# Expert products as three float32r products, with the weights split into a high and a low part on the chip

## Chip, cores and metric

The kernel runs on one core of one Trainium2 chip. The metric is the device time of one execution, in microseconds (us), lower is better.

## The reference, cut to what matters

One layer: attention (4 sequences of 1024 tokens, 256 features, 16 heads of 16), and behind it a mixture of eight experts of which each token takes two, with a layer norm before and behind each half.

```python
x = x + _layernorm(attention(_layernorm(x), Wq, bq, Wk, bk, Wv, bv, Wo, bo))
xs = _layernorm(x).reshape(4096, 256)
dist = sqrt(max(|xs|^2 + |centroid|^2 - 2 xs @ centroid.T, 1e-12))
w, sel = top_k(dist, 2); w = softmax(w)             # we: (4096, 8), zero but for the chosen two
for e in range(8):                                  # Wg, W1: 256 x 684, W2: 684 x 256
    h = silu(xs @ Wg[e] + bg[e]) * (xs @ W1[e] + b1[e])
    out = out + we[:, e:e+1] * (h @ W2[e] + b2[e])
x = x + _layernorm(out)
```

All inputs and the output are float32.

## The kernel before, in words

Every engine runs its own written-out program; semaphores order them, and nothing is reordered. The stages follow one another: layer norm and q, k, v projections; attention; the output projection with both norms and the routing distances; the routing; the experts; the last norm.

**Attention** goes over 16 groups (batch and four heads), and a group over 16 units. For every unit PE makes four score products for the row maxima of a *later* group (`max_scores`, L1547, five units ahead), four score products for the softmax (`scores`, L1561), both in float32r, and `weigh` (L1574, float32). DVE reduces the maxima (`reduce_max`, L970 and L977), two halves of 1024 columns a unit. After eight units (half r of a group) the maxima are complete: POOL splits them (`split_max`: a cast L776, a subtraction L778), and DVE turns the result (`turn`, L983). `turn(g, 0)` stands in DVE's order between two reductions:

```python
            def max_pass(g, first=False):
                for m in range(UNITS):
                    reduce_max(g, m, 0)
                    if m == 0 and not first:
                        turn(g - 1, 1)
                    if m == ST:
                        turn(g, 0)
                    reduce_max(g, m, 1)
```

POOL's program in a group g is: `split_max(g + 1, 0)`, `split_max(g + 1, 1)`, `copy_values` for group g + 2 (L767; it waits until group g is weighed, so it runs some units into group g + 1), and in the groups 9 and 13 `norm_o` (two multiplications of 128 x 1024, L797) behind that. SP issues all DMAs of a group in a written-out order: the last result, the stacks and values of group g + 2, the rows of maxima of group g + 1, and at the end of the group's list a load that the later stages need (first weights `load_w1`, second weights `load_w2`).

**Projection and norms**: 16 steps of 256 rows; `norm_o` (L797) for batch 3 stands between two of POOL's additions `add_y` (L841), and waits for loads from `ot_scr` and `r_scr` that SP issues at step 4. PE's `project_o` waits for `norm_o`.

**Experts**: 71 tiles of 128 rows, each of one expert, whose number is read from `tile_e`. All weights and biases lie in SBUF. For a tile t, POOL gathers 128 rows (L852) and their weights (L866). PE turns the rows (`turn_rows`, L1703), makes gate and up (`gate_up`: four quarters of 342 columns, each of two float32 products, L1717), turns the 128 x 684 hidden values (`turn_hidden`, six transposes of 114 columns, L1727) and multiplies by the second weights (`down`, six float32 products of 256 columns, L1736). The trace has two MATMUL records for each float32 product, one for each float32r product and one for each transpose. DVE adds biases (L1208, L1211) and multiplies (L1216), ACT takes the silu (L1443), both save the turned hidden values (ACT L1454, DVE L1227), ACT scales the result (`save_y`, L1449), and POOL scatters it with addition into `y_d` (L859). PE's order in the loop is `gate_up(t)`, `turn_rows(t + 1)`, `down(t - 1)`, `turn_hidden(t)`.

**The last norm** reads `y_d` and a part of `x2_d` back: SP issues all twelve loads and only then reports the first (`s_back`), for which DVE's statistics (L1281) wait.

## Time and profile before

| | |
|---|---|
| runs of the kernel before | 1572.35, 1585.21, 1585.65 us; median 1585.21 us |
| the profiled execution | 1571.72 us, of it span 1569.9 us |
| mean granted TensorE clock | 0.956 |
| PE busy | 1428.5 us (91%) |
| DVE, ACT, POOL busy | 1107.7, 833.7, 430.8 us |
| moved by DMA | 141.82 MB, mean 90 GB/s |

The span is the time from the first to the last instruction. Busy times are sums over the engine's instructions; a PE that is busy by its records is not at its peak. PEld is the loading of stationary operands, which runs beside PE.

### The profile page before, as it was taken

To read this page: it belongs to the slowest core of one execution; us is meant where nothing else is said; L and a number is where in the kernel's file an instruction comes from. 1 tells how busy PE (TensorE), PEld (TensorE's weight loads), DVE (VectorE), ACT (ScalarE), POOL (GpSimd) and SP (SyncE) were. 2 spreads that over 40 slices of the span, in tenths; PEclk is the share of its full clock that TensorE was granted. 3 is DMA by queue.
4 is the path that set the end of the run, shared out by engine and by line. 5 is a ranking of instruction groups with operands and counts; after the bars stand their busy time and mean duration, and the time that the engine had idled before them with its cause. 6 is when DMAs were issued, how large, how long until landed. Compare 5 with 4: busy or idle time off the path is not lost.

```text
span 1569.9 us, 30203 instructions
## 1 busy us (share of the span) xinstructions
PE 1428.5 (91%) x9419; PEld 813.8 (52%) x9420; DVE 1107.7 (71%) x2101; ACT 833.7 (53%) x1613; POOL 430.8 (27%) x417
## 2 busy tenths in 40 slices
PE   7899999999999999999999259999999999999950
PEld 5454334333343433333455136777777777777740
DVE  6988999999999989997047764555554545555425
ACT  4523888888888878887956322222222222222215
POOL 5750000000000010001024143444444444444425
PEclk9998999999999999998999669999999999999985
DMA  6986274334646454540558804211221122122235
GB/s 209 257 225 116 69 171 98 59 81 68 96 64 126 65 90 65 94 79 16 159 91 204 281 25 95 33 30 33 33 33 33 31 33 33 30 33 33 33 92 193
DMA packets 125118, 141.82 MB, mean 90 GB/s; under 512 B 55131, under 2 KB 98949, under 8 KB 125030
## 3 DMA queue, kind: packets, MB, share of 16 engines
q1 hardware_dynamic: 109126, 121.98, 33.7%
q0 software_dynamic: 15904, 18.66, 7.2%
q8 instruction: 56, 0.92, 0.3%
q14 instruction: 32, 0.26, 0.1%
HBM read 86.30 MB, written 54.30 MB: 90 GB/s over the span
## 4 chain that ended last, share of the span: by engine, by line
PE 53%; DVE 36%; issue 6%; DMA 1%; POOL 1%; ACT 1%; SPq 1%; DVEq 0%; POOLq 0%; ACTq 0%
DVE mx L977 26%; PE psum L1717 21%; PE psum L1736 12%; DVE psum L970 4%; PE psum L1574 4%; PE psum L1547 3%; PE psum L1727 3%; PE psum L1561 2%; PE psum L1648 2%; PE psum L1521 1%; PE psum L1646 1%; PE psum L1507 1%; PE psum L1703 1%; PE psum L1667 1%; DVE work L1176 1%
## 5 line engine op out<-in xcount | busy, mean ns | idle before, releaser
L1366 ACT ACTIVATE work<-psum 128x512 f32<-128x512 f32 x1024 | 543.5, 600 | 92.1 <-PE psum L1561 67.1
L977 DVE TENSOR_REDUCE mx<-psum 128x1 f32<-128x1024 f32 (+1 forms) x512 | 547.2, 1097 | 23.6 <-PE psum L1547 10.5
L1547 PE MATMUL psum<-stack 48*128 48x512 f32 x1024 | 378.6, 451 | 19.6 <-DVE mx L977 8.8
L1561 PE MATMUL psum<-stack 50*128 50x512 f32 x1024 | 376.8, 453 | 0.0
L1717 PE MATMUL psum<-weights,values 128*128 x1136 | 340.6, 454 | 0.6 <-DVE values L1196 0.6
L1574 PE MATMUL psum<-work,values 128*32 128x384 f32 x4080 | 304.2, 394 | 0.2
L1547 PEld LDWEIGHTS psum<-stack 48*128 48x128 f32 x1024 | 162.7, 188 | 260.1 <-DVE mx L977 169.3
L1717 PEld LDWEIGHTS psum<-weights,values 128*128 128x128 f32 x1136 | 211.6, 191 | 98.8 <-issue 2.8
L1443 ACT ACTIVATE values<-values 128x342 f32<-128x342 f32 x142 | 69.3, 488 | 253.7 <-DVE values L1208 253.7
L1736 PE MATMUL psum<-weights,work 114*128 (+1 forms) x852 | 198.6, 383 | 1.1 <-ACT work L1454 0.8
L1561 PEld LDWEIGHTS psum<-stack 50*128 50x128 f32 x1024 | 162.4, 188 | 23.9 <-ACT work L1366 18.6
L1736 PEld LDWEIGHTS psum<-weights,work 114*128 114x128 f32 (+1 forms) x852 | 158.0, 192 | 21.1 <-issue 1.7
L1574 PEld LDWEIGHTS psum<-work,values 128*32 128x32 f32 x4080 | 89.4, 109 | 125.5 <-issue 103.3
L852 POOL DMA_INDIRECT values<-xn_d,at_x x71 | 70.0, 986 | 280.1 <-DVE at_w L1239 274.6
L1449 ACT ACTIVATE work<-psum,dots 128x256 f32<-128x256 f32 x71 | 33.6, 473 | 197.6 <-PE psum L1736 193.0
L1208 DVE TENSOR_TENSOR values<-psum,work 128x342 f32<-128x342 f32 x142 | 73.1, 515 | 92.3 <-PE psum L1717 64.2
L859 POOL DMA_INDIRECT y_d<-work,at_y x71 | 115.2, 1622 | 40.0 <-issue 27.2
L1211 DVE TENSOR_TENSOR values<-psum,work 128x342 f32<-128x342 f32 x142 | 73.1, 515 | 61.3 <-PE psum L1717 61.3
L1227 DVE COPY work<-psum 114x256 f32<-114x256 f32 x71 | 30.2, 425 | 117.8 <-PE psum L1727 117.8
L776 POOL CAST m<-mx 128x16 fp32r<-128x16 f32 x32 | 6.3, 198 | 365.4 <-DVE mx L977 365.4
L1216 DVE TENSOR_TENSOR values<-values 128x342 f32<-128x342 f32 x142 | 73.3, 516 | 14.7
L767 POOL TENSOR_TENSOR values<-weights,dots 128x512 f32<-128x512 f32 x16 | 20.5, 1283 | 227.0 <-issue 226.8
(185 smaller groups left out, 1266.8 us busy)
## 6 DMA issues: line engine op xcount, KB each, us to landing
stack<-qk_scr SPq DMA_DIRECT2D x192, 128.0 KB, 6.2
qk_scr<-weights SPq DMA_DIRECT2D x16, 1024.0 KB, 4.8
weights<-in_w SPq DMA_DIRECT2D x8, 1368.0 KB, 6.9
ot_scr<-weights SPq DMA_DIRECT2D x16, 512.0 KB, 3.2
weights<-in_w SPq DMA_DIRECT2D x8, 684.0 KB
work<-in_b SPq DMA_DIRECT2D x8, 684.0 KB, 8.7
y_d<-zeros SPq DMA_DIRECT2D x1, 4224.0 KB, 14.2
v_scr<-weights SPq DMA_DIRECT2D x32, 128.0 KB, 2.4
```

The costliest lines, as they stand in the source:

```text
L852: pool.indirect_dma_start(out=x_row, out_offset=None, in_=xn2_d, in_offset=bass.IndirectOffsetOnAxis(ap=at_x[:, 0:1], axis=0)).then_inc(s_ ...
L859: pool.indirect_dma_start(out=y_d, out_offset=bass.IndirectOffsetOnAxis(ap=at_y[:, 0:1], axis=0), in_=y_row, in_offset=None, compute_op=AL ...
L977: dve.tensor_reduce(mx[:, r, a, t:t + 1], scored, AX, ALU.max, negate=True).then_inc(s_max, 1)
L1208: dve.tensor_tensor(gates[c], bank(2 * c)[:, 0:CH], bias(0), ALU.add).then_inc(s_gb, 1)
L1211: dve.tensor_tensor(hid[:, CH * c:CH * (c + 1)], bank(2 * c + 1)[:, 0:CH], bias(HID), ALU.add).then_inc(s_ub, 1)
L1216: dve.tensor_tensor(hid[:, CH * c:CH * (c + 1)], hid[:, CH * c:CH * (c + 1)], gates[c], ALU.mult).then_inc(s_hid, 1)
L1366: act.activation(pt[u % 4][:, j, :], bank((c + HG * u + n) % 3), ACT.Exp, scale=SC).then_inc(s_exp, 1)
L1547: ins = pe.matmul(bank(4 + 2 * a + half), qs[t3][at:at + QROWS, r, P * t:P * (t + 1)], ks[t3][at:at + QROWS, r, 512 * half:512 * (half + 1 ...
L1561: pe.matmul(bank((t3 + HG * u + n) % 3), ks[t3][at:at + MROWS, r, P * st:P * (st + 1)], qs[t3][at:at + MROWS, r, 512 * half:512 * (half + ...
L1574: last = pe.matmul(bank(3)[32 * j:32 * (j + 1), lo:hi], vg[p][:, st, j, :], pt[u % 4][:, j, lo:hi], start=st == 0 and lo == 0, stop=st == ...
L1717: last = pe.matmul(dst, x_t[:, k, :], w1_sb[:, bass.ds(e, 1), k, col:col + CH].rearrange("p a n -> p (a n)"), start=k == 0, stop=k == KC - 1)
L1736: last = pe.matmul(bank(7)[:, 0:C], h_t[0:rows, k, :], w2_sb[0:rows, bass.ds(e, 1), k, :].rearrange("p a n -> p (a n)"), start=k == 0, sto ...
```

## The change

Every float32 product of the experts becomes three float32r products, high x high, high x low and low x high, where the high part of a number is its float32r rounding and the low part the rest.

- **First weights.** In attention, SP loads the raw weights of an expert n (`load_expert`, in group `SPLIT_AT[n]`: the weights and, spread over all partitions, their last row), in the next group the bias row, and in the group after that stores the parts to DRAM (`store_expert`, six high parts and four low ones). POOL makes the parts in the group between (`split_weights`: two subtractions of the last row, two casts, two subtractions, each of 128 x 1368), behind `copy_values` and ahead of the next group's `split_max`. The bias is the last of the 256 rows, and the last feature of every row of x is the number one: since a normed row sums to zero, its last feature is expressed by the others. Half of `xn2_d` is preset to ones for it, and `keep` stores 255 columns.
- In the projection stage SP stores `x2` in eight parts and loads high parts of the experts 0 and 1 (steps 2 and 3, ahead of the loads that `norm_o` waits for), then low parts, then the other high parts; those of expert 7 during the first tiles. PE's first tile waits for all but expert 7.
- **Second weights** no longer lie in SBUF: SP loads them for each tile (`load_w2`, three DMAs, 684 rows of 1 KB and the bias row), ACT makes the high part (`high_w2`, 128 x 1536) and DVE the low part (`low_w2`).
- **A tile** has 24 float32r products of 342 columns and 18 of 256, in place of 8 and 6 float32 ones; two and six transposes as before (now of up to 128 columns). The bias additions on DVE are gone; the silu reads PSUM. ACT makes the high parts of x and of the hidden values, DVE the low ones. Gathered rows have two buffers.
- **The last norm**: `x2` is loaded back during the last tiles, and SP issues four loads of `y_d` and reports the first before it issues more.

The diff, cut to its core (blank lines left out):

```diff
-KH, KP = 6, HID // 6
+KH = -(-HID // P)
+LAST = HID - (KH - 1) * P
+SPLIT_ORDER = (4, 5, 6, 7, 0, 1, 2, 3)
+SPLIT_AT = (0, 1, 3, 5, 7, 9, 11, 13)
...
         stack_shape = [P, 2, PAIRS, T]
...
+        total = w1_size + 12288
         first_stack = placed("stack0", stack_shape, F32R, w1_size + 640)
         other_stacks = [placed(f"stack{n + 1}", stack_shape, F32R, total + stack_at * n) for n in range(2)]
         stack = [first_stack] + other_stacks
+        w_hi = placed("w_hi", [P, E, KC, 2 * HID], F32R, w1_size)
...
+        def load_expert(sp, n):
+            e, p = SPLIT_ORDER[n], n % 2
+            if 2 <= n:
+                sp.wait_ge(s_wst, 16 * (2 * min(n - 1, 4) + max(n - 5, 0)))
+            if n == E - 1:
+                sp.wait_ge(s_split, split_steps(E - 2, 1))
+            sp.dma_start(split_raw[split_in[n]][:, :, :], w1[e].rearrange("(k p) n -> p k n", p=P)).then_inc(s_raw[p], 16)
+            sp.dma_start(last_row[n], w1[e, C - 1, :].partition_broadcast(P)).then_inc(s_raw[p], 16)
+        def load_bias_row(sp, n):
+            p = n % 2
+            sp.wait_ge(s_raw[p], 48 * (n // 2) + 32)
+            sp.dma_start(split_raw[split_in[n]][P - 1:P, KC - 1, :], b1[SPLIT_ORDER[n]].rearrange("(a n) -> a n", a=1)).then_inc(s_raw[p], 16)
+        def store_expert(sp, n):
+            sp.wait_ge(s_split, split_steps(n, 3))
+            sp.dma_start(wh_d[SPLIT_ORDER[n]], w_hi[:, high_in[n], :, :].bitcast(F32)).then_inc(s_wst, 16)
+            if n < 4:
+                sp.dma_start(wl_d[SPLIT_ORDER[n]], w_lo[:, split_in[n], :, :].bitcast(F32)).then_inc(s_wst, 16)
+        def load_high(sp, e, done=s_w):
...
+        def load_w2(sp, t, p):
+            after(sp, s_w2l, t - 1)
+            e = sp.value_load(tile_e[0:1, bass.ds(t, 1)], min_val=0, max_val=E - 1)
+            src = w2[bass.ds(e, 1), :, :].rearrange("a r n -> (a r) n")
+            sp.dma_start(w2_raw[p][:, 0:KH - 1, :], src[0:P * (KH - 1), :].rearrange("(k p) n -> p k n", p=P)).then_inc(s_w2[p], 16)
+            sp.dma_start(w2_raw[p][0:LAST, KH - 1, :], src[P * (KH - 1):HID, :]).then_inc(s_w2[p], 16)
+            sp.dma_start(w2_raw[p][LAST:LAST + 1, KH - 1, :], b2[bass.ds(e, 1), :]).then_inc(s_w2[p], 16)
...
+                for n, at in enumerate(SPLIT_AT):
+                    if g == at + 2 and n < E - 2:
+                        store_expert(sp, n)
+                    if g == at + 1:
+                        load_bias_row(sp, n)
+                    if g == at:
+                        load_expert(sp, n)
+                if g == 12:
+                    load_wo(sp)
+                elif g == 2:
+                    sp.dma_start(xn2_d.rearrange("(n p) d -> p n d", p=P)[:, :, P:C],
+                                 ones_f[:, :].rearrange("p (a d) -> p a d", a=1).to_broadcast([P, NT, P])).then_inc(s_yc, 16)
+                elif g == 4:
                     sp.dma_start(y_d.rearrange("(n p) d -> p n d", p=P),
...
+            def split_weights(n):
+                p, at, raw, high = n % 2, split_in[n], split_raw[split_in[n]], w_hi[:, high_in[n], :, :]
+                pool.wait_ge(s_raw[p], 48 * (n // 2 + 1))
+                for k in range(KC):
+                    rows = P - k // (KC - 1)
+                    part = raw[0:rows, k, :]
+                    pool.tensor_tensor(part, part, last_row[n][0:rows, :], ALU.subtract).then_inc(s_split, 1)
+                for k in range(KC):
+                    pool.wait_ge(s_split, split_steps(n, 1) if n == E - 1 else split_steps(n, 0) + k + 1)
+                    pool.tensor_copy(high[:, k, :], raw[:, k, :]).then_inc(s_split, 1)
+                for k in range(KC):
+                    pool.wait_ge(s_split, split_steps(n, 1) + k + 1)
+                    pool.tensor_tensor(w_lo[:, at, k, :], raw[:, k, :], high[:, k, :].bitcast(F32), ALU.subtract).then_inc(s_split, 1)
...
+                for n, at in enumerate(SPLIT_AT):
+                    if g == at + 1:
+                        split_weights(n)
                 if g in (9, 13):
...
+            def low_x(t):
+                dve.wait_ge(s_xh, t + 1)
+                dve.tensor_tensor(x_lo[:, :, :].rearrange("p k t -> p (k t)"), bank(6)[:, 0:C],
+                                  x_hi[:, :, :].rearrange("p k t -> p (k t)").bitcast(F32), ALU.subtract).then_inc(s_mx, 1)
...
             def multiply(t, c):
                 dve.wait_ge(s_si, 2 * t + c + 1)
...
-                dve.tensor_copy(at_x[:, :], token_of[:, bass.ds(t, 1)]).then_inc(s_ig, 1)
+                dve.wait_ge(s_gu, 4 * t + 2 * c + 2)
+                part = hid[:, CH * c:CH * (c + 1)]
...
+            def low_hidden(t):
+                dve.wait_ge(s_hh, t + 1)
+                dve.tensor_tensor(h_lo[:, :, :].rearrange("p k t -> p (k t)"), bank(4, 2)[:, 0:KH * P],
+                                  h_hi[:, :, :].rearrange("p k t -> p (k t)").bitcast(F32), ALU.subtract).then_inc(s_hl, 1)
+            def low_w2(t, p):
+                dve.wait_ge(s_w2h, t + 1)
+                dve.tensor_tensor(w2_lo[:, :, :], w2_raw[p], w2_hi[:, :, :].bitcast(F32), ALU.subtract).then_inc(s_w2l, 1)
...
+            def tile(t, p):
+                first = isinstance(t, int) and t == 0
+                if not first:
+                    low_hidden(t - 1)
+                multiply(t, 0)
+                if not first:
+                    low_w2(t - 1, 1 - p)
+                multiply(t, 1)
+                if not isinstance(t, int) or t + 1 < NS:
+                    low_x(t + 1)
+                    keep_weight(t + 1)
+                if not isinstance(t, int) or t + 3 < NS:
+                    aim_gather(t + 3, 1 - p)
+                if not isinstance(t, int) or t + 2 < NS:
+                    aim_weight(t + 2)
+                if not first:
+                    aim_scatter(t - 1)
...
+            def gate(t, c):
+                act.wait_ge(s_gu, 4 * t + 2 * c + 1)
+                act.activation(hid[:, CH * c:CH * (c + 1)], bank(2 * c)[:, 0:CH], ACT.Silu).then_inc(s_si, 1)
+            def high_x(t):
+                act.wait_ge(s_mt, t + 1)
+                act.activation(x_hi[:, :, :].rearrange("p k t -> p (k t)"), bank(6)[:, 0:C], ACT.Copy).then_inc(s_xh, 1)
+            def high_hidden(t):
+                act.wait_ge(s_ht, t + 1)
+                after(act, s_yp, t)
+                act.activation(h_hi[:, :, :].rearrange("p k t -> p (k t)"), bank(4, 2)[:, 0:KH * P], ACT.Copy).then_inc(s_hh, 1)
+            def high_w2(t, p):
+                act.wait_ge(s_w2[p], 48 * ((t - p) // 2 + 1) if isinstance(t, int) else 24 * (t - p) + 48)
+                after(act, s_yp, t)
+                act.activation(w2_hi[:, :, :].rearrange("p k n -> p (k n)"), w2_raw[p].rearrange("p k n -> p (k n)"),
+                               ACT.Copy).then_inc(s_w2h, 1)
...
+            def tile(t, p):
+                first = isinstance(t, int) and t == 0
+                if not first:
+                    high_hidden(t - 1)
+                gate(t, 0)
+                if not first:
+                    high_w2(t - 1, 1 - p)
+                gate(t, 1)
+                if not isinstance(t, int) or t + 1 < NS:
+                    high_x(t + 1)
+                if not first:
...
+            def down(t):
                 after(pe, s_yr, t)
-                for k in range(KH):
-                    rows = KP + 1 if k == 0 else KP
...
+                for n, (h, w, ready, of_w) in enumerate(((h_hi, w2_hi, s_hh, s_w2h), (h_lo, w2_hi, s_hl, s_w2h), (h_hi, w2_lo, s_hh, s_w2l))):
+                    pe.wait_ge(ready, t + 1)
+                    pe.wait_ge(of_w, t + 1)
+                    for k in range(KH):
+                        rows = P if k < KH - 1 else LAST + 1
+                        last = pe.matmul(bank(7)[:, 0:C], h[0:rows, k, :], w[0:rows, k, :],
+                                         start=n + k == 0, stop=(n, k) == (2, KH - 1))
                 last.then_inc(s_yp, 1)
...
+            def tile(t, p):
+                gate_up(t)
+                if not isinstance(t, int) or t + 1 < NS:
+                    turn_rows(t + 1, 1 - p)
+                if not (isinstance(t, int) and t == 0):
+                    down(t - 1)
+                turn_hidden(t)
             pe.wait_ge(s_slot, 1)
...
+                        pe.matmul(dst, x_hi[:, k, :], columns(w_hi, k, col), start=k == 0, stop=False)
+                        pe.matmul(dst, x_hi[:, k, :], columns(w_lo, k, col), start=False, stop=False)
+                        last = pe.matmul(dst, x_lo[:, k, :], columns(w_hi, k, col), start=False, stop=k == KC - 1)
                     last.then_inc(s_gu, 1)
```

## Rows read from the trace of the kernel before

**Rows 1.** Chain of waits, 1200 to 1215 us: start, length, what.

```profile
1203.90 4.60 PE psum L1717 x16
1208.50 0.22 PE psum L1703 x2
1208.72 2.59 PE psum L1736 x12
1211.31 0.66 PE psum L1727 x6
```

**Rows 2.** Chain of waits, 200 to 230 us, by line.

```profile
by line: DVE mx L977 86.4%; DVE psum L970 12.3%; issue 3.3%; DVEq L974 0.4%; DVE m_t L983 0.4%; DVEq L80 0.1%
```

**Rows 3.** Timeline, PE in attention, PEld in a tile: start, length, engine, line.

```profile
401.74 0.40 PE L1547 MATMUL psum<-stack 48*128 48x512 f32 x1
401.98 0.39 PE L1547 MATMUL psum<-stack 48*128 48x512 f32 x1
...
1202.86 0.79 PEld L1727 LDWEIGHTS psum<-ident,values 128*114 128x114 f32 x6
```

**Rows 4.** Groups of instructions by line, POOL: count, busy us, mean ns, idle before.

```profile
L797 POOL TENSOR_TENSOR weights<-weights 128x1024 f32<-128x1024 f32 x8 | 18.8, 2370 | 0.3 <-DMA weights<-r_scr 0.3
L776 POOL CAST m<-mx 128x16 fp32r<-128x16 f32 x32 | 6.3, 198 | 365.4 <-DVE mx L977 365.4
L829 POOL CAST weights<-weights 128x128 f32<-128x128 int32 x1 | 0.3, 291 | 0.1
```

**Rows 5.** Timeline of POOL, groups 8 and 9 of attention (idle before in brackets).

```profile
509.71 1.28 POOL L767 TENSOR_TENSOR values<-weights,dots 128x512 f32<-128x512 f32 x1 [16.10 <-issue]
513.03 0.20 POOL L776 CAST m<-mx 128x16 fp32r<-128x16 f32 x1 [2.03 <-DVE mx L977]
...
549.44 1.28 POOL L767 TENSOR_TENSOR values<-weights,dots 128x512 f32<-128x512 f32 x1 [16.09 <-issue]
550.68 4.72 POOL L797 TENSOR_TENSOR weights<-weights 128x1024 f32<-128x1024 f32 x2
555.33 0.21 POOL L776 CAST m<-mx 128x16 fp32r<-128x16 f32 x1
```

**Rows 6.** Timeline of DVE at the turn that follows.

```profile
555.88 0.21 DVE L983 STREAM_TRANSPOSE m_t<-m 128x32 f32<-128x32 f32 x1 [2.18 <-POOL m L778]
```

**Rows 7.** Stretches: busy us of PE, PEld, DVE, ACT, POOL; PEclk, DMA share, GB/s.

```profile
558.00:560.00 2.00, 2.00 (x14) 0.83 (x6) 1.44 (x3) 0.88 (x2) 0.00 (x0) 0.55 1.02 131
...
722.00:724.00 2.00, 2.00 (x22) 1.23 (x22) 1.49 (x3) 1.18 (x3) 0.00 (x0) 0.51 0.05 8
...
730.00:732.00 2.00, 2.00 (x18) 1.08 (x18) 1.08 (x3) 0.98 (x3) 0.00 (x0) 0.50 0.00 0
```

**Rows 8.** Groups by line, ACT and DVE, same columns as rows 4.

```profile
L1336 ACT ACTIVATE weights<-work 128x1024 fp32r<-128x1024 f32 x16 | 16.9, 1056 | 29.8 <-POOL work L747 28.0 <-DMA qk_scr<-weights 1.7
L1443 ACT ACTIVATE values<-values 128x342 f32<-128x342 f32 x142 | 69.3, 488 | 253.7 <-DVE values L1208 253.7
...
L1216 DVE TENSOR_TENSOR values<-values 128x342 f32<-128x342 f32 x142 | 73.3, 516 | 14.7
L1160 DVE TENSOR_TENSOR weights<-weights 128x568 f32<-128x568 f32 x1 | 0.8, 752 | 0.0
```

**Rows 9.** Timeline of a tile, scatter and multiplication; and from the scatter's line.

```profile
1205.49 1.62 POOL L859 DMA_INDIRECT y_d<-work,at_y  x1 [0.30 <-issue]
...
1206.97 0.52 DVE L1216 TENSOR_TENSOR values<-values 128x342 f32<-128x342 f32 x1
...
DMA to landing us min/median/max: 3.6/3.8/9.8
```

**Rows 10.** Timeline of POOL in the projection stage.

```profile
842.76 4.65 POOL L797 TENSOR_TENSOR weights<-weights 128x1024 f32<-128x1024 f32 x2
```

**Rows 11.** Timeline of the last norm: SP's loads, DVE's first statistics.

```profile
1520.53 2.85 SPq L690 DMA_DIRECT2D weights<-y_d  x5
...
1534.07 0.75 DVE L1281 BATCH_NORM_STATS2 dots<-weights 128x6 f32<-128x256 f32 x2 [18.35 <-SPq L699]
```

More of the change, by code:

```diff
@@ L96, in cuts, with split_steps @@
     return sum(cut(n, 1) for n in range(m))
+def split_steps(n, parts):
+    return KC * (3 * n + parts)
 def groups(eng, body):
@@ L318, in build @@
         c = Carve(weights)
+        x2_again = c.take([NT, C])
         y_all = c.take([NT, C])
@@ L396, in build @@
         s_ys = sem("expert_out_stored")
-        s_gt = [sem(f"rows_gathered{i}") for i in range(8)]
+        s_gt = [sem(f"rows_gathered{i}") for i in range(4)]
         s_back = sem("rows_back")
@@ L683, in _ @@
-            load_b1(sp, E - 1, s_last)
-            load_w2(sp, E - 1, s_last)
-            load_w1(sp, E - 1, s_last)
+            sp.wait_ge(s_wd, 32)
+            sp.wait_ge(s_slot, 1)
+            sp.wait_ge(s_rpad, 3)
+            for t in range(2):
+                load_w2(sp, t, t)
+            load_low(sp, E - 1, s_last)
+            load_high(sp, E - 1, s_last)
+            with sp.Fori(1, (NS - 5) // 2) as i:
+                for p in range(2):
+                    load_w2(sp, 2 * i + p, p)
@@ new lines, in _ @@
+            for t in range(NS - 5, NS):
+                load_w2(sp, t, t % 2)
+                if t >= 2 * NT + 2:
+                    for m in ((0, 1), (2, 3, 4), (5, 6, 7))[t - 2 * NT - 2] if t < 2 * NT + 5 else ():
+                        sp.wait_ge(s_gu, 4 * (2 * NT + (1024 * m + 1023) // (KC * 2 * HID)))
+                        sp.dma_start(x2_again[:, 4 * m:4 * m + 4, :],
+                                     x2_d.rearrange("(n p) d -> p n d", p=P)[:, 4 * m:4 * m + 4, :]).then_inc(s_x2r, 16)
@@ L696, in _ @@
+            for m in range(4):
+                load_y(m)
             for m in range(NT // 4 + 2):
                 if m < NT // 4:
-                    sp.wait_ge(s_gt[m], 32 if 4 * m >= kept else 16)
+                    sp.wait_ge(s_gt[m % 4], 16 * (m // 4 + 1))
                     sp.sem_inc(s_back, 4)
+                    if m + 4 < NT // 4:
+                        load_y(m + 4)
                 if m < 2:
@@ L1264, in _ @@
-            tiles(2, NT)
-            dve.wait_ge(s_last, 48)
-            tiles(NT, NS - 2)
-            for t in range(NS - 2, NS):
-                hidden(t)
-                if t + 1 < NS:
-                    save_xt2(t + 1)
-                aim_scatter(t - 1)
-                save_ht(t)
+                tile(t, t)
+            with dve.Fori(1, (NS - 3) // 2) as i:
+                for p in range(2):
+                    tile(2 * i + p, p)
+            for t in range(NS - 3, NS):
+                tile(t, t % 2)
@@ L1273, in _ @@
+            low_hidden(NS - 1)
+            low_w2(NS - 1, (NS - 1) % 2)
             aim_scatter(NS - 1)
@@ L1449, in save_y @@
                 act.activation(y_row, bank(7)[:, 0:C], ACT.Copy, scale=w_all[:, bass.ds(t, 1)]).then_inc(s_yr, 1)
-            def save_ht(t):
-                act.wait_ge(s_ht, t + 1)
-                after(act, s_yp, t)
-                act.activation(h_t.rearrange("p k t -> p (k t)")[0:KP, 0:4 * P], bank(4)[0:KP, :], ACT.Copy).then_inc(s_hta, 1)
-            gate(0)
-            save_ht(0)
-            gate(1)
-            save_y(0)
-            save_ht(1)
-            with act.Fori(2, NS) as t:
-                gate(t)
-                save_y(t - 1)
-                save_ht(t)
+            def tile(t, p):
[9 more added lines that the diff above has]
+                if not first:
+                    save_y(t - 1)
+            high_x(0)
+            for t in range(2):
+                tile(t, t)
+            with act.Fori(1, (NS - 1) // 2) as i:
+                for p in range(2):
+                    tile(2 * i + p, p)
+            tile(NS - 1, (NS - 1) % 2)
+            high_hidden(NS - 1)
+            high_w2(NS - 1, (NS - 1) % 2)
             save_y(NS - 1)
@@ L1769, in layout @@
+            for t in range(2):
+                tile(t, t)
+            def tiles(lo, hi):
+                with pe.Fori(lo, hi) as i:
+                    for p in range(2):
+                        tile(2 * i + p, p)
+            tiles(1, NT // 2)
+            pe.wait_ge(s_last, 32)
+            tiles(NT // 2, (NS - 1) // 2)
+            tile(NS - 1, (NS - 1) % 2)
+            down(NS - 1)
 def layout(inputs):
```

331 lines of the change are left out of this document (139 added, 192 removed).

## Prediction, made before the change was run

> **What bounds the kernel now.** I read the chain of waits first, then timelines of the two stages that hold most of the time. In the expert stage the chain is PE and nothing else: 4.60 us of gate and up, 0.22 of row turns, 2.59 of the second product, 0.66 of hidden turns [rows 1], a period of 8.07 us and 71 x 8.07 = 573 us in all. What makes PE shorter there shortens the kernel, until ACT and DVE come up. In attention the chain is DVE's maxima, 86% + 12% [rows 2]; PE runs just beside it. There a wait of DVE costs its full length. The change works in both: it relieves PE in the first, and gives POOL, which splits the maxima for DVE, long work in the second.
>
> **The expert stage, gain.** A float32 product is two records, of 4.60 / 16 = 0.288 us at 342 columns and 2.59 / 12 = 0.216 us at 256 [rows 1]: at the granted clock of 1.0 (2.4 GHz) that is two passes over the columns per record, four per product. The nearest row for a float32r product, L1547, has a single record for 512 columns, and two start 0.24 us apart [rows 3]; one pass at 2.4 GHz is 0.213. So I take one pass: 342 / 2.4 = 0.143, with the 0.002 by which the records above exceed their passes 0.145; by the 0.24 of rows 3 it would be 0.160. At 256 columns one pass is 0.107, and the load of the stationary operand, once per product, sets the pace: six transposes, each with its load, take 0.66, or 0.110 each [rows 1]; the loads by themselves show 0.79 / 6 = 0.131 [rows 3]. PE then has 24 x 0.145 + 18 x 0.110 + 0.22 + 0.66 = 3.48 + 1.98 + 0.88 = 6.34 us a tile; by the dear ends 3.84 + 2.36 + 0.88 = 7.08. That a 128-row operand streams as the 48-row one does is the assumption.
>
> The load rule bears on this. The Trainium skill (TensorE: Matmul & The Clock Gate, section LDWEIGHTS) gives the load as columns / 1.2, which is 107 ns for 128 columns: three quarters of the 342-column pass and all of the 256-column one. By it the second product would stand at its limit, 18 x 0.107; by the 0.110 it is 0.05 us a tile more.
>
> **Can ACT and DVE follow?** From the start of a tile: ACT makes the high part of the hidden values (1056 ns x 768 / 1024 = 0.79 [rows 8]); the first quarter of gate and up is there at 6 x 0.145 = 0.87, about 1.17 with its drain; silu 0.49 [rows 8] ends at 1.66; `high_w2` of 1536 columns is 1.5 x 1.056 = 1.58, to 3.24; `low_w2` on DVE is 0.752 + 968 x (0.752 - 0.516) / 226 = 1.76 [rows 8], to 5.0; the second multiplication 0.52, to 5.5. PE asks for it when it comes to `turn_hidden`, at 3.48 + 0.22 + 1.98 = 5.68. All hidden, but by 0.2 us only. DVE's operations of a tile add up to under 5 us (0.96 for the low hidden part and 1.76, 2 x 0.52, 0.42 for x by the same slope, and small ones); POOL's three DMAs are as before. The second weights have two buffers and nearly two periods from request to use; their 700 KB a tile are hidden, and what they can disturb is the scatter's landing, 3.8 us from issue [rows 9], on which `save_y` waits with about 0.3 us to spare. So I take 6.45, with 6.34 and 7.1 as ends: 71 x (8.07 - 6.45) = 115 us gained (123 to 69). Filling and draining have two more steps at the first and last tile: 3 us lost.
>
> A rule speaks against it. In rows 9 a DVE multiplication of two SBUF operands (L1216) begins and ends, at its usual 0.52, inside a scatter's 1.62 us on POOL. The Trainium skill (SBUF — State Buffer, the passage on engine ports) says that a GpSimd operation that reads SBUF and a DVE operation with two SBUF inputs hold the shared port pair exclusively. `low_w2` is such an operation of 1.76 us. By the row nothing is added; by the rule up to 1.76 us would be added to either engine in each tile.
>
> **Attention, loss.** `split_weights` is six POOL operations. The subtractions are 4 x 2.37 x 1368 / 1024 = 12.7 us at most [rows 4], about 12.3 if a fixed 0.2 us is taken off before scaling. The casts cost 0.198 us for 16 columns and 0.291 for 128 [rows 4], so 0.83 ns a column and 1.3 us each for 1368; no row shows a long cast, and a subtraction's 3.1 is the upper end. I take 1.5: 12.3 + 3.0 = 15.3 us (15.0 to 18.8).
>
> Where they stand decides. `split_weights(n)` is behind `copy_values` and ahead of the next group's first `split_max`. `copy_values` ends at 509.71 + 1.28 = 510.99 and the maxima's cast begins at 513.03 [rows 5]: POOL has 2.04 us there, not the 16 it has elsewhere. Queued behind the long work are the cast and subtraction of the maxima; DVE waits for them in `turn`, with the next reductions behind it; PE waits for DVE's banks, and with it everything. The trace has the case in small. In group 9, `norm_o` (4.72 us) stands in the same place: the cast begins at 555.33 in place of 549.44 + 3.32 = 552.76, 2.57 late [rows 5], and DVE idles 2.18 us for POOL L778 [rows 6]. So all but 0.39 of a delay reaches DVE. What follows adds to it: the granted clock falls to 0.55 at 558, and after the other `norm_o` (group 13) it is 0.51 to 0.50 for the five stretches from 722 to 732 [rows 7], its lower level, 1.2 GHz, at which PE is the slower engine. Half of 3 to 10 us at that level is 1.5 to 5; I take 2.4.
>
> One collision costs 15.3 - 2.04 - 0.39 + 2.4 = 15.3 us (14.1 to 21.4). The splits fall in the groups 1, 2, 4, 6, 8, 10, 12 and 14; behind the one of 14 no maxima follow. Seven collisions: 107 us lost (99 to 150; the upper end needs the dear cast each time, and I use 130).
>
> SP's new DMAs in attention (eight loads, eight bias rows, ten stores) stand at the end of its list, where it idles until the next group; POOL's wait for the bias row has been met by then. Hidden; if not, the delay adds to the same wait.
>
> **The rest.** In the projection stage, `norm_o` of batch 3 begins at 842.76 [rows 10] without a wait, but 2.8 MB of high parts and two parts of x2 now go ahead of its loads. At the 131 GB/s of a full DMA share [rows 7] 2.8 MB are 21 us, and part is absorbed by the queue's slack, which I can't see: 0 to 12, taken 5 us lost. At the end, SP's first load is issued at 1520.53 and DVE starts at 1534.07 [rows 11], 13.5 later; with four loads issued (about 2.85 us [rows 11]) and one landing (3.8, as the scatter's [rows 9]) it is 6.7, so 7 us gained (4 to 9).
>
> **The sum.** -115 + 3 + 107 + 5 - 7 = -7 us against the profiled execution of 1571.7: 1565. That execution is at the low end of the three runs (1572.35 to 1585.65, median 1585.21), which spread by 0.85% with nothing changed; I name 1569, a little toward the middle. That is no change: within 1% is about what a measurement of this kernel can tell from none, on either side.
>
> **Rivals.**
> - *The gain prevails.* PE reaches 6.34, the cast is cheap, the DMAs of the projection stage are hidden: -123 + 3 + 99 + 0 - 8 = -29, 1543 us. For it: ACT and DVE have the time by rows 8; against it: 0.2 us of slack.
> - *Slower: the tile is paced by the chain high part, low part, multiplication.* If anything adds 0.2 us to `high_w2` or `low_w2` (DVE and POOL meeting at the port, a late scatter ahead of ACT's next tile), every further 0.1 us costs 7 us. At 7.1 us a tile and 120 for attention: -69 + 3 + 120 + 8 - 6 = +56, 1628 us; it turns slower than before from 6.55 us a tile on.
> - *Float32r doesn't stream in one pass on 128 rows*, so a product costs what a float32 record does: 24 x 0.288 + 18 x 0.216 + 0.88 = 11.7 us a tile, +257 us and the 107 of attention, above 1900 us. Only the 0.24 of rows 3 speaks against it, and that clearly enough.
> - *The change does what it says*, the split is hidden in attention and only the gain is left: 1450 to 1460 us. Rows 5 and 6 speak against it.
>
> **How the numbers follow.** The forecast 0.42, the gain prevails 0.27, slower by the tile's chain or dearer stalls 0.25, two passes 0.03, hidden split 0.03. The forecast's own range is 1550 to 1592. The whole range takes in both neighbours up to 1 in 10 on each side: 1537 to 1622. Faster by over 1%: 0.27 + 0.03 and a little of the forecast's lower edge, 0.32; slower by over 1%: 0.25 + 0.03 and some of its upper edge, 0.30; within 1%: 0.38.
>
> **What would show each step.** Attention lasts about 107 us longer; DVE idles seven times for some 13 us before its turn of the maxima, put down to POOL's subtraction, and the granted clock falls to 0.5 behind each; the split's subtractions take 3.1 us, its casts 1.3 to 1.6. The tile's period in the chain of waits is 6.3 to 6.5 and all PE; if DVE or ACT lines appear in it, the rival is at work. PE's records are 42 float32r ones a tile, with starts 0.145 and 0.110 apart. DVE's first statistics of the last norm start 7 us after SP's first load. I am wrong if POOL's long operations are much faster than the scaled row, if the clock stays low long after a stall, or if the tile's chain is not PE's.

## The result and the profile after

| | before | after |
|---|---|---|
| median, us (range) | 1578.78 (1571.06 to 1585.65) | 1673.68 (1669.57 to 1676.76) |
| ratio to before | | 1.061, 95% interval 1.056 to 1.066 |
| profiled execution, us | 1571.7 | 1676.8 |
| granted clock, mean | 0.956 | 0.919 |

The forecast was 1569 us, no change, in a range of 1537 to 1622. The kernel is 6% slower. By stages of the two profiled executions:

| stage | before | after | difference | forecast |
|---|---|---|---|---|
| attention, to the store of its last output | 792.9 | 902.9 | +110.1 | +107 |
| projection and routing, to the first row turns | 135.5 | 150.3 | +14.7 | +5 |
| expert tiles, to the end of the last product | 585.6 | 576.0 | -9.6 | -112 |
| last norm | 55.9 | 44.8 | -11.1 | -7 |

One term decides, the gain in the tiles. Chain of waits after, inside the tiles (start, length, what); it answers to [rows 1]:

```profile
1299.94 2.63 PE psum L1862 x14
1302.56 0.81 PE psum L1852 x6
1303.37 0.16 PE psum L1842
1303.53 0.16 PE psum L1843
...
1307.15 0.22 PE psum L1826 x2
1307.37 3.10 PE psum L1862 x18
1310.47 0.81 PE psum L1852 x6
1311.28 0.16 PE psum L1842
```

The chain is PE alone, as forecast, but a tile takes 7.91 us (1303.37 to 1311.28 on the chain), not 6.45. (Four of the 70 periods are 8.8 us; in those PE waits 0.7 us for the high part of the second weights.) A gate or up product takes 0.157 us (forecast 0.145), the 18 products of `down` 3.10 (1.98), the hidden turns 0.81 (0.66, though there are still six). The timeline of PE's loads in the same tile:

```profile
1307.10 0.97 PEld L1862 LDWEIGHTS psum<-w_hi,h_hi 128*128 128x128 f32 x6
1308.20 0.97 PEld L1862 LDWEIGHTS psum<-w_hi,h_lo 128*128 128x128 f32 x6
1309.30 0.97 PEld L1862 LDWEIGHTS psum<-w_lo,h_hi 128*128 128x128 f32 x6
1310.40 0.60 PEld L1852 LDWEIGHTS psum<-ident,values 128*128 128x128 f32 x6
```

Six loads are spread over 0.97 us, 0.156 apart on average, and each six takes 1.10. With 342 columns at 0.157 and 256 at 0.156, my first reading was that the load of a full stationary operand sets one pace for all float32r products. It was wrong: 0.156 is an average over uneven distances, as the experiments show.

POOL's timeline at the first collision in attention, then DVE's; they answer to [rows 5, 6]:

```profile
232.34 6.18 POOL L884 TENSOR_TENSOR split_raw<-split_raw 128x1368 f32<-128x1368 f32 x2
238.44 2.61 POOL L887 CAST w_hi<-split_raw 128x1368 fp32r<-128x1368 f32 x2
241.00 6.10 POOL L890 TENSOR_TENSOR w_lo<-split_raw,w_hi 128x1368 fp32r<-128x1368 f32 x2
247.03 0.22 POOL L854 CAST m<-mx 128x16 fp32r<-128x16 f32 x1
247.32 0.22 POOL L856 TENSOR_TENSOR m<-mx,m 128x16 f32<-128x16 f32 x1
```
```profile
247.57 0.21 DVE L1090 STREAM_TRANSPOSE m_t<-m 128x32 f32<-128x32 f32 x1 [12.24 <-POOL m L856]
```

The split takes 14.7 us and DVE idles 12.24 for it. The stretches of 2 us show the clock behind it (PEclk is the column of two decimals after POOL's), which answers to [rows 7]:

```profile
238.00:240.00 2.00, 0.00 (x0) 0.00 (x0) 0.00 (x0) 0.00 (x0) 2.00 (x3) 1.00 1.07 141
242.00:244.00 2.00, 0.00 (x0) 0.00 (x0) 0.00 (x0) 0.00 (x0) 2.00 (x1) 0.50 1.04 137
258.00:260.00 2.00, 2.00 (x12) 0.66 (x11) 1.37 (x2) 0.70 (x2) 0.00 (x0) 0.50 0.00 0
262.00:264.00 2.00, 1.92 (x18) 0.71 (x18) 1.51 (x3) 1.40 (x3) 0.00 (x0) 1.00 0.01 4
```

PE is empty in the first two, stands at 0.50 (1.2 GHz) from 242 to 260, and is back at 1.00 at 262. Seven copies of the values with a split behind them lie 54.2 to 57.2 us from the next copy, most of the others 39.7: 14.5 to 17.5 us each, 111 in all.

Projection and the last norm; POOL's row answers to [rows 10], SP's and DVE's to [rows 11]:

```profile
961.54 4.64 POOL L875 TENSOR_TENSOR weights<-weights 128x1024 f32<-128x1024 f32 x2 [8.49 <-DMA weights<-r_scr]
```
```profile
1634.29 7.43 SPq L767 DMA_DIRECT2D weights<-y_d  x7
...
1638.44 0.75 DVE L1381 BATCH_NORM_STATS2 small<-weights 128x6 f32<-128x256 f32 x2 [12.20 <-SPq L775]
```

`norm_o` of the last batch now waits 8.49 us for its inverses. DVE starts the last norm 4.2 us after SP's first load, in place of 13.5. The costs of a tile's new operations, from the page's groups, answer to [rows 8]:

```profile
L1317 DVE TENSOR_TENSOR h_lo<-psum,h_hi 128x768 fp32r<-128x768 f32 x71 | 68.0, 958 | 171.1 <-ACT h_hi L1551 171.1
L1322 DVE TENSOR_TENSOR w_lo<-work,w_hi 128x1536 fp32r<-128x1536 f32 x36 | 63.1, 1752 | 1.5 <-ACT w_hi L1556 0.8 <-issue 0.7
L1551 ACT ACTIVATE h_hi<-psum 128x768 fp32r<-128x768 f32 x71 | 57.6, 812 | 10.4 <-PE psum L1852 7.2
L1556 ACT ACTIVATE w_hi<-work 128x1536 fp32r<-128x1536 f32 x36 | 53.3, 1480 | 0.0
```

### The profile page after: what moved, and what is told of

The parts are those of the page before. It is cut to its first block, busy times and chain, and to the rows that moved or that the text cites. A ratio compares the mean times of both kernels' runs of the same rounds, so it can differ in the third digit from the quotient of the medians.

```text
span 1674.0 us, 31840 instructions
## 1 busy us (share of the span) xinstructions
PE 1444.0 (86%) x10413; PEld 893.7 (53%) x10414; DVE 1112.5 (66%) x1890; ACT 968.4 (58%) x1755; POOL 548.2 (33%) x464
## 4 chain that ended last, share of the span: by engine, by line
PE 50%; DVE 25%; issue 13%; POOL 7%; DMA 2%; SPq 2%; ACT 1%; DVEq 0%; POOLq 0%; ACTq 0%
DVE mx L1084 17%; PE psum L1862 13%; PE psum L1844 5%; PE psum L1842 5%; PE psum L1843 5%; PE psum L1697 4%; PE psum L1670 4%; PE psum L1852 3%; POOL split_raw L884 3%; PE psum L1684 2%; DVE psum L1077 2%; PE psum L1630 2%; PE psum L1644 1%; POOL w_lo L890 1%; PE psum L1771 1%
## 5 line engine op out<-in xcount | busy, mean ns | idle before, releaser
L1842 PE MATMUL psum<-w_hi,x_hi 128*128 x568 | 188.4, 332 | 1.0 <-DVE x_lo L1302 1.0
L1844 PE MATMUL psum<-w_hi,x_lo 128*128 x568 | 182.4, 321 | 0.0
L1317 DVE TENSOR_TENSOR h_lo<-psum,h_hi 128x768 fp32r<-128x768 f32 x71 | 68.0, 958 | 171.1 <-ACT h_hi L1551 171.1
L1843 PE MATMUL psum<-w_lo,x_hi 128*128 x568 | 181.6, 320 | 0.0
L1313 DVE TENSOR_TENSOR values<-values,psum 128x342 f32<-128x342 f32 x142 | 72.0, 507 | 85.3 <-PE psum L1844 78.5
L955 POOL DMA_INDIRECT y_d<-values,at_y x71 | 115.2, 1622 | 41.0 <-issue 28.1
L1842 PEld LDWEIGHTS psum<-w_hi,x_hi 128*128 128x128 f32 x568 | 108.0, 190 | 2.4 <-issue 1.7
L1843 PEld LDWEIGHTS psum<-w_lo,x_hi 128*128 128x128 f32 x568 | 108.3, 191 | 0.0
L1844 PEld LDWEIGHTS psum<-w_hi,x_lo 128*128 128x128 f32 x568 | 107.8, 190 | 0.0
L1542 ACT ACTIVATE values<-psum 128x342 f32<-128x342 f32 x142 | 64.7, 456 | 62.4 <-PE psum L1844 57.3
```

What stands on the lines that cost most here:

```text
L955: pool.indirect_dma_start(out=y_d, out_offset=bass.IndirectOffsetOnAxis(ap=at_y[:, 0:1], axis=0), in_=y_row, in_offset=None, compute_op=AL ...
L1313: dve.tensor_tensor(part, part, bank(2 * c + 1)[:, 0:CH], ALU.mult).then_inc(s_hid, 1)
L1842: pe.matmul(dst, x_hi[:, k, :], columns(w_hi, k, col), start=k == 0, stop=False)
L1843: pe.matmul(dst, x_hi[:, k, :], columns(w_lo, k, col), start=False, stop=False)
L1844: last = pe.matmul(dst, x_lo[:, k, :], columns(w_hi, k, col), start=False, stop=k == KC - 1)
```

## The experiments

Apart from the kernel with everything together, these were single executions, each with a profile, so they are read by stage: "tiles" is the time from the first row turns to those of tile 70, over 70 periods. It is 8.15 before and 7.94 after. Whole times of kernels that keep the split where it was are a poor measure: attention ended up to 20 us apart in them, with DVE's idle for POOL the same, 89.8 to 90.0 us. The granted clock between 100 and 300 us was 0.92 after the change, 0.93 in the kernel with two result rows (attention 7 us shorter) and 0.77 in the one with 64 stationary columns (13 us longer).

### First group: where the split stands, and what paces a product

**Split in the gap** of attention:

```diff
                 if not (isinstance(g, int) and g + 1 >= NG):
-                    for r in range(PAIRS):
-                        split_max(g + 1, r)
+                    split_max(g + 1, 0)
+                for n, at in enumerate(SPLIT_AT):
+                    if g == at + 2:
+                        split_weights(n)
+                if not (isinstance(g, int) and g + 1 >= NG):
+                    split_max(g + 1, 1)
                 if not (isinstance(g, int) and g + 2 >= NG):
                     copy_values(i, c + 2)
-                for n, at in enumerate(SPLIT_AT):
-                    if g == at + 1:
-                        split_weights(n)
```

> POOL splits the same weights one group later, between the two splits of the maxima, where it idles 19 us. If the seven collisions behind the copy of the values made the 110 us of attention, attention ends at 793 to 797 us again in place of 902.9 and the run is near 1567; the split's six operations still take 14.7 us. The rival is that the split costs by what it does beside other engines (its port, its loads and stores), wherever it stands: then attention stays within 20 us of 903.

1566.6 us. Attention ended 110.6 us earlier than after the change and 0.5 earlier than before it; the split's operations are as long (POOL, this kernel):

```profile
242.56 6.24 POOL L890 TENSOR_TENSOR w_lo<-split_raw,w_hi 128x1368 fp32r<-128x1368 f32 x2
253.23 0.20 POOL L854 CAST m<-mx 128x16 fp32r<-128x16 f32 x1 [4.43 <-DVE mx L1085]
```

POOL ends the split and idles 4.43 us for DVE, where DVE idled 12.24 for POOL. The split costs by its place alone; its loads, stores and port cost nothing that shows.

**Full rows** in `down`:

```diff
-                        rows = P if k < KH - 1 else LAST + 1
+                        rows = P
```

> The second product's last chunk runs with all 128 rows (its padding is zero times one) in place of 45. In the kernel as changed, six products with loads 0.156 us apart are followed by the next six 1.10 us after them, so the short one takes about 0.32. If the change of the row count costs the 0.16, a tile's three times six products fall from 3.25 to 2.8, the period from 7.90 to 7.4 to 7.5, and the run by 28 to 33 us. If the 0.16 belongs to something else (the switch between operands, the wait on the low part), the period stays at 7.9.

1636.9 us, tiles 7.44, as expected, but the sixes fell by more, and what they gained is partly lost in a wait. PE's loads and products in one tile:

```profile
1303.69 0.78 PEld L1862 LDWEIGHTS psum<-w_hi,h_hi 128*128 128x128 f32 x6
1304.40 0.79 PEld L1862 LDWEIGHTS psum<-w_hi,h_lo 128*128 128x128 f32 x6
```
```profile
1304.51 0.88 PE L1862 MATMUL psum<-w_hi,h_lo 128*128 128x256 f32 x6
1306.08 0.95 PE L1862 MATMUL psum<-w_lo,h_hi 128*128 128x256 f32 x6 [0.69 <-DVE w_lo L1322]
1306.87 0.82 PE L1852 MATMUL psum<-ident,values 128*128 128x128 f32 x6
```

Six products take 0.71 to 0.72 us in place of 1.10, so one takes 0.12, less than the 0.156 that I had taken for the pace of a load. And a new bound has come up: in this tile the third six wait for `low_w2`, which was the slower rival of the forecast. It is every second tile that waits; the periods alternate between 6.8 and some 8.2 us.

**256 moving columns** in gate and up:

```diff
-                    return w[:, bass.ds(e, 1), k, col:col + CH].rearrange("p a n -> p (a n)")
+                    return w[:, bass.ds(e, 1), k, col:col + 256].rearrange("p a n -> p (a n)")
...
-                    dst = bank(c)[:, 0:CH]
+                    dst = bank(c)[:, 0:256]
```

> Gate and up products have 256 moving columns in place of 342 (it leaves out a quarter of the gate and up columns). Theory: the load of the 128-column stationary operand paces a float32r product, 0.156 us at either width; then the 24 products stay at 3.7 to 3.8 us a tile and the period at 7.9. Rival: the moving columns stream slower than one a cycle at 2.4 GHz (342 columns in 0.156 us are 0.46 ns each); then a product takes 0.117 us, the 24 take 2.8 and the period is 6.9 to 7.0, the run 65 us shorter.

1643.2 us. Products are 0.119 us apart: my theory of the load fell, the rival had the product right. Its period of 6.9 to 7.0 holds in every second tile only (tiles 7.48: PE now waits for `low_w2` here too). The load of a short product in this run and the one behind it; their products start at 1302.97 and 1303.29:

```profile
1302.97 0.18 PEld L1862 LDWEIGHTS psum<-w_hi,h_lo 45*128 45x128 f32 x1
1303.28 0.19 PEld L1862 LDWEIGHTS psum<-w_lo,h_hi 128*128 128x128 f32 x1
```

The load of the short operand starts with its product, not one product ahead, and so does the next full one.

**64 stationary columns** in `down`:

```diff
-                        last = pe.matmul(bank(7)[:, 0:C], h[0:rows, k, :], w[0:rows, k, :],
+                        last = pe.matmul(bank(7)[0:64, 0:C], h[0:rows, k, 0:64], w[0:rows, k, :],
```

> The second product has 64 of the 128 stationary columns (it leaves out the second half of each tile's tokens in that product). Theory: the load sets its pace; half the columns take half the load, and a product falls from 0.156 us to its 256-column pass, 0.107 to 0.115; the 18 take 2.1 to 2.3 us in place of 3.25 and the period is 6.9 to 7.1. Rival: the load is not what sets it (the row count, or a fixed cost of a float32r product); then products stay 0.156 apart and the period at 7.9.

1671.4 us, tiles 7.64. The load shrank from 189 to 135 ns (45 rows: 183 to 129), full products stayed 0.12 apart, and a six fell from 1.10 to 0.99:

```profile
1306.73 1.09 PE L1862 MATMUL psum<-w_hi,h_hi 128*64 128x256 f32 x6
1307.74 1.05 PE L1862 MATMUL psum<-w_hi,h_lo 128*64 128x256 f32 x6
```

That is 2 x 0.054 saved in each six: two loads in each lie bare, that of the 45-row operand and the one behind it. Neither theory had that.

### Second group: what is late next

All four take full or equal rows, and this order, in which the weights' parts are made ahead of the silus (ACT) and multiplications (DVE):

```diff
-                gate(t, 0)
                 if not first:
                     high_w2(t - 1, 1 - p)
+                gate(t, 0)
...
-                multiply(t, 0)
                 if not first:
                     low_w2(t - 1, 1 - p)
+                multiply(t, 0)
```

> The full rows of the earlier run, and ACT takes the high part of the second weights ahead of both silus, DVE their low part ahead of both multiplications. With full rows PE waited 1.1 us a tile on DVE's low part of the second weights. Theory: that wait is all that kept PE at about 7.4 us; a product costs 0.46 ns a moving column (24 x 0.157 + 18 x 0.120 + 0.22 + 0.81 = 6.96), so the period is 6.95 to 7.05 and the chain PE alone, the run 28 us below the one with full rows. Rival: the chain of high part, low part and multiplication holds the tile in either order; then ACT and DVE lines stay in the chain and the period stays above 7.2.

**Full rows and the order:** 1625.9 us, 11 less than with full rows alone, not 28. In the first 38 tiles the theory held, with a chain of PE alone (to 1288 us) and a period of 6.80 us behind the first two; from 1306 us on, periods of 6.8 and of 8.8 to 9.9 alternate, 7.9 on average. The first three rows are a tile near the end of the good part, the rest a loop of two tiles later:

```profile
1278.62 0.22 PE psum L1826 x2
1278.83 2.16 PE psum L1862 x18
1280.99 0.66 PE psum L1852 x6
...
1297.72 6.98 DMA y_d<-values,at_y
1304.72 0.05 ACTq L1563
...
1305.89 1.48 ACT w_hi L1556
1307.37 0.70 ACT values L1542 x2
...
1309.08 0.83 DVE values L1313 x2
...
1313.79 6.82 DMA y_d<-values,at_y
```

The scatter takes 6.5 to 7.0 us from issue to landing ([rows 9] had 3.8). `save_y` waits for it with its one buffer, behind `save_y` stands ACT's next tile, behind that DVE's, at whose end the next scatter is aimed. The loop is 15.6 to 16.1 us long. The prediction had named this landing as what the weights' loads can disturb. The hidden turns are back at 0.66, so the 0.15 was the load behind the last 45-row product.

**115 rows throughout**, and **114 rows with one chunk of 115** (`rows = KP + 1`, and `rows = KP + k // (KH - 1)`, with KP = HID // KH = 114, the second weights loaded in chunks of 114 rows):

> Six hidden chunks of 114 values, each product with 115 rows, each transpose with 114 columns, and the order of the run before it. Theory: what costs is that the load of an operand with another size is not laid beside the product ahead of it; with equal sizes products stay 0.120 apart at 115 rows, transposes 0.110, and the period is 3.77 + 2.16 + 0.22 + 0.66 = 6.81. Rival: any row count under 128 costs; then the 18 products are slower than with full rows and the period is above 7.2.

> As the run with 115 rows, but five chunks of 114 rows and one of 115. If any change of the row count lays the loads bare (theory 1), the loads on both sides of the 115-row product show again, about 0.37 us each six, and the period is 7.8 to 7.9 (or 7.3 if only one side shows). If what matters is which block of 32 rows or which half of the array is used (theory 2: 45 rows are fewer blocks than 128, 114 and 115 are the same), the period is 6.8, as with 115 rows throughout.

1680.4 and 1692.4 us, tiles 8.06 and 8.09: as times both expectations missed, because the chain went into a gather. It is mostly the slot weights', of 3.8 to 5.9 us (2.3 before the change), beside second weights that are now loaded in 114 rows; why that gather is slow beside that shape, and not beside 128 rows, stays open. What they were made for can be read at clock 1.00. With 115 rows throughout, sixes start at 1319.72, 1320.44 and the turns at 1321.16, 0.72 apart. With 114 and 115:

```profile
1501.15 0.88 PE L1861 MATMUL psum<-w_hi,h_lo 114*128 114x256 f32 x6
1501.88 0.88 PE L1861 MATMUL psum<-w_lo,h_hi 114*128 114x256 f32 x6
1502.60 0.82 PE L1851 MATMUL psum<-ident,values 128*114 128x128 f32 x6
```

0.72 to 0.73 again. Fewer rows than 128 cost nothing, and a change by one row costs nothing; 128 to 45 costs. By blocks of 32 rows these are 4 and 4 against 4 and 2, which fits theory 2; where between 45 and 114 the line lies was not tried, nor was a stream of 45 rows alone. Few rows by themselves don't lay a load bare: in attention before the change, products of 48 rows start at 401.74 and 401.98 [rows 3], 0.24 us apart at 512 columns, and the load between them runs beside the first (a second stream, of 50 rows, runs beside this one):

```profile
401.74 0.19 PEld L1547 LDWEIGHTS psum<-stack 48*128 48x128 f32 x1
```

**456 moving columns** (three chunks in place of four, with the silus and multiplications cut to fit):

```diff
-                for c in range(4):
-                    col = (c % 2) * HID + (c // 2) * CH
-                    dst = bank(c)[:, 0:CH]
+                for c in range(3):
+                    col = c * WIDE
+                    dst = bank(c)[:, 0:WIDE]
...
```

> Gate and up in 18 products of 456 columns in place of 24 of 342, full rows and the same order. Theory: 0.46 ns a moving column and nothing fixed worth naming, so 18 x 0.208 = 3.74 us in place of 24 x 0.157 = 3.77 and a period within 0.05 of the run with full rows and that order. Rival: a fixed part per product (the load, at 342 columns) is in the 0.157; then wide products cost 0.193 each, 3.47 in all, and the period is 0.3 us shorter.

1624.6 us, 1.3 from the kernel with 342: starts at 1249.99 and 1250.19, 0.205 on average over six. Three widths stand on a line: 0.119 at 256, 0.157 at 342, 0.205 at 456, some 0.43 ns a column and 0.01 us fixed. The good tiles took 6.75 us, within the 0.05 of the theory; then it fell into the same slow loop.

### Third group: the loop, the projection stage, and everything together

**Two result rows** (beside full rows and the order): `y_row` and `at_y` have two buffers, and only POOL waits for the scatter before.

```diff
-            def scatter(t):
+            def scatter(t, p):
...
+                after(pool, s_ys, 16 * t)
...
-                after(act, s_ys, 16 * t)
+                after(act, s_ys, 16 * (t - 1))
```

> Full rows and the new order, and two buffers for a tile's result rows and their destinations, so that ACT and DVE no longer wait for the scatter before; GpSimd alone does. With one buffer the period was 6.77 us, PE alone, up to 1288 us and then 7.95, with a loop over two tiles that holds a scatter of 6.8 to 7.0 us from issue to landing (3.8 before the change). Theory: that loop is what holds the second half; without it the period is 6.8 to 6.9 to the end and the run is 38 to 42 us below the one with one buffer, at 1584 to 1590. Rival: the transfers themselves are too slow beside 700 KB of second weights a tile, and the loop closes elsewhere (the gathers, the weights' high part); then the run stays above 1610.

1586.7 us, tiles 6.81 to the end:

```profile
1406.13 0.22 PE psum L1827 x2
1406.35 2.15 PE psum L1863 x18
1408.49 0.66 PE psum L1853 x6
1412.93 0.22 PE psum L1827 x2
```

39 us less than with one buffer: the loop through the scatter is what held the second half.

**High parts later**, and **stores of x2 later too**:

```diff
-                if u in (2, 3):
-                    load_high(sp, u - 2)
+                if u in (6, 7):
+                    load_high(sp, u - 6)
```
```diff
-                if u % 2 == 1:
-                    store_x2(u // 2)
+                if u >= 8:
+                    store_x2(u - 8)
```

> In the projection stage SP issues its two loads of split high parts behind the loads of the last batch (steps 6 and 7 in place of 2 and 3). If those loads made the last batch's rows late, the wait of 8.49 us of POOL's norm falls to nothing and PE's of 8.19 us with it, and the stage is 10 to 12 us shorter, the run at 1662 to 1668. If the last batch's rows were late for another reason (the stores of x2 and of the kept rows), the stage stays at 150 us.

> As the run with the high parts loaded later, and the stores of x2 begin at step 8 in place of step 1, behind the loads of the last batch. With the high parts alone moved, POOL's last norm still waited 3.2 us (8.5 before it) and the stage from the end of attention to the first row turns fell from 147.6 to 145.1 us. If the x2 stores hold the rest, the wait is 0 to 0.5 and the stage 140 to 143 us. If the stage is full of transfers that were there before the change, the wait stays at 3 us and the stage at 145, or the stage is given back at the first gather, behind the later transfers.

1676.4 and 1668.3 us. The first expectation missed: the norm's wait fell from 8.49 to 3.23 us only, and the stage from POOL's first constant to the first row turns from 147.6 to 145.1 us. With the stores moved too the norm waits for nothing and the stage is 137.8 us (132.9 before the change). Nine other kernels here leave this stage as the change made it; in them it took 145.7 to 152.3 us, and the norm waited 4.4 to 10.1. The 137.8 is clear of this spread and the 145.1 lies at its edge; the last kernel below, which moves the high parts alone, had 142.6. So both together held some 10 of the 14.7 us, and how it divides between them isn't shown. Of the 4.9 left, 2.2 are the first gather's, whose landing takes 5.1 us in place of 3.0; the rest was not tried.

Little of this reached the whole time. With the stores moved the tiles took 564.4 us in place of 556.0: ten tiles were of the 8.8 us kind, against four after the change. Whether the later stores cause that, a single execution can't say.

**All together** (the split and the two norms of attention in the gap, high parts later, full rows, the order, two result rows):

> All that helped together: the split between the two splits of the maxima, the two norms of attention in the same gap (groups 10 and 14), high parts loaded later, full rows, the new order, two result rows. By the theories the parts add up: 1585 less 110 (attention) less 12 (projection stage) less 5 to 10 (the two norms) is 1455, range 1440 to 1480, ratio to the kernel before 0.92 to 0.93. If the shorter tiles collide with their transfers again, it ends above 1490.

1471.6 us (1467.2 to 1487.1), ratio to the kernel before 0.935, interval 0.930 to 0.940, in six executions against eleven. Tiles 6.79, attention to POOL's first constant 787.6 us (795.5 before), stage 142.6. It is 17 us above my sum. Beside the kernel with two result rows (1586.7, where the sum started from 1585), attention ended 110.7 us earlier, where I had 115 to 120 for the split and the two norms, and the stage was 5.1 us shorter, where I had 12. That kernel's attention had ended 7 us earlier than the changed kernel's, so less was left to gain.

## Why the prediction was wrong

- **What bounds the kernel:** right. PE alone in the tiles, DVE in attention.
- **Attention +107:** right, +110.1. The split is 14.7 us (15.3 forecast; the cast 1.3, not 1.5), DVE idles 12.2, and 3.7 on average are left (111 / 7 less 12.2) where I took 2.4 for the clock. That this rest is the clock is read from the 0.50 behind the collision, and no run separates it. That only the place costs is shown by the split in the gap.
- **Gate and up, 24 x 0.145:** mis-sized by +0.30 us a tile, 21 us in all. It came from counting one pass at 2.4 GHz; the 0.24 us of 512 columns in [rows 3] by itself would have given the 0.160 that I named and did not take. The 256-, 342- and 456-column runs show 0.119, 0.157 and 0.205.
- **The step that failed: 18 x 0.110 for `down`, six turns at 0.66.** I priced all 18 alike, from six transposes with equal operands [rows 1]. Three of the 18 have 45 rows, and on either side of each the load lies bare: six loads of 0.18 to 0.19 us, 1.09 us a tile, 77 us in all. Shown by full rows (1.10 to 0.72 a six, 0.81 to 0.66 in the turns), by half the stationary columns (the six shrinks by twice what the load does), and by 114 and 115 rows (nothing). The kernel before had chunks of 114 and 115 rows; the change brings the 45, and my list of what it adds left that out. Full products take 0.120, 0.18 us a tile more than forecast. 6.34 + 0.30 + 1.09 + 0.18 = 7.91. Why a load overlaps between equal operands and not across this change is not shown; that it doesn't is.
- **Loads.** A load record of these products is 189 ns at 128 columns and 135 at 64, and hidden in a stream of equal operands. The Trainium skill (TensorE: Matmul & The Clock Gate, LDWEIGHTS) gives 107 ns for 128 columns, which I had set beside the row's 0.110; the measurement decides. The same page of the Trainium skill says (Part 3: Packing small matmuls, what overlaps and what doesn't) that a load overlaps a product in flight only where the two differ in row group; its passage on the mechanism also lets a load into a background buffer go ahead. The first of the two doesn't hold here: 128 after 128 rows overlaps, 45 after 128 does not. The measurement decides.
- **ACT and DVE follow, "by 0.2 us only":** right at 7.91 us a tile, where the second multiplication ended 5.6 us after the tile's first product (5.5 forecast). But the check compared it with `turn_hidden` at 5.68 and passed over an earlier need: by its own terms the third six of `down` ask for `low_w2` at 3.48 + 0.22 + 12 x 0.110 = 5.02 us, and it was to end at 5.0. At PE's 6.8 it fails in every second tile: in the tile shown under full rows `low_w2` ended 6.2 us after the first product (4.9 in the tile before it), and with the order changed the scatter's loop came up. So the forecast's 6.45 would hardly have been reached in this order whatever the products cost; that is an inference. Why DVE's first multiplication began 4.0 us after the first product there, 2.2 in the tile before it and 3.0 in the changed kernel, I can't say. No port effect shows: `low_w2` takes 1.75 to 1.76 us and POOL's scatter 1.62, whether they meet or not.
- **Projection +5, last norm -7:** +14.7 and -11.1. The transfers were the right place, for some 10 us of the 14.7; the whole was beyond my bound of 12, and I had counted the stores of x2 with the high parts.
- **Rivals:** "slower by the tile's chain" had the side right (1628) and the mechanism wrong: PE itself was slow. Its mechanism is real and appears as soon as PE is mended. "The change does what it says" (1450 to 1460) needed all the edits of the last kernel, and was then measured at 1471.6.

## What to carry to other kernels

Count the shapes of the operands, not only the products: a last chunk of few rows in a stream of full ones can cost more than it saves, and padding it with zero rows costs nothing. Long background work on an engine that also serves the critical path belongs where that engine waits for the path, and one place in the order can be worth 110 us with the same instructions. After an engine is made faster, look for the loop that is right behind it (here one buffer and a scatter's landing, 7.9 us a tile, where PE had taken 7.91) before believing the gain.

## What the runs showed of the hardware

At a granted clock of 1.00 a float32r product took 0.119, 0.157 and 0.205 us at 256, 342 and 456 moving columns, where one record of a float32 product at 342 columns took 0.288. Its load of 128 columns is a record of 189 ns and hides behind the product before, also at 114 or 115 rows, but not across a change from 128 to 45 rows or back. After PE had stood empty for 12 us the granted clock was 0.50 from 242 to 260 us, 11 us beyond PE's return at 249. A tile stage could run at 6.80 us a tile for 258 us and then at 7.9 with the same instructions; two buffers in place of one ended that, and what tipped it over at that tile isn't shown. Beside the second weights' loads of each tile a scatter landed in 6.5 to 7.0 us, 3.8 before the change.
